# Three unread products beside each score transpose, in the stretch before the experts

## The reference, cut to what matters

```
x = layernorm(x + attention(x))                       # 16 heads, causal, 8 x 112 rows of 512
x = layernorm(x + gated_linear_attention(x, ctx))     # 8 x 375 context rows
logits = x @ router_weight.T + router_bias            # 8 experts
top_vals, top_idx = top_k(logits, 2)
scores = zeros.at[row, top_idx].set(softmax(top_vals))
act = (clip(up, -7, 7) + 1) * gate * sigmoid(1.702 * gate)      # per expert, 512 -> 2 x 512
expert_out = act @ down_proj[e] + down_proj_bias[e]             # 512 -> 512
out = sum over e of scores[:, e] * expert_out[e]
x = layernorm(x + out)
```

## Time and profile before

| | us |
|---|---|
| median of 3 runs | 919.36 |
| lowest and highest | 916.23, 919.87 |
| the profiled execution, its own time | 918.16 |
| its span, first to last instruction | 916.4 |
| TensorE busy in the span | 850.3 (93%) |
| mean granted TensorE clock | 0.964 |

### The profile page before, as it was taken

How to read it: one execution, slowest core, us unless ns; L and a number is a source line. 1 busy time by engine, 2 the same in 40 slices (tenths; PEclk the granted TensorE clock), 3 DMA queues, 4 the chain that set the end, 5 groups by cost and what they waited for, 6 DMA issues and landing times.

```text
span 916.4 us, 12580 instructions
## 1 busy us (share of the span) xinstructions
PE 850.3 (93%) x4967; PEld 743.9 (81%) x4967; DVE 470.6 (51%) x853; ACT 307.6 (34%) x666; POOL 105.6 (12%) x95
## 2 busy tenths in 40 slices
PE   6999999999999999899999999989988899999980
PEld 6999998989898989878898777777737888888760
DVE  4435454453636352756732335444665576666524
ACT  4343323141423332512542212221233355554420
POOL 0000000000000000000000001000131144444333
PEclk9999999999999999999999999999958899999995
DMA  9940725431200103004100101100564366655326
GB/s 327 351 161 1 236 77 188 126 123 64 87 6 25 69 1 116 1 6 167 35 1 1 34 34 58 58 1 24 217 231 120 122 188 187 190 154 165 72 30 184
DMA packets 34461, 96.99 MB, mean 106 GB/s; under 512 B 5720, under 2 KB 7768, under 8 KB 31712
## 3 DMA queue, kind: packets, MB, share of 16 engines
q1 hardware_dynamic: 30592, 87.70, 27.8%
q0 software_dynamic: 3808, 8.46, 4.6%
HBM read 64.03 MB, written 32.12 MB: 105 GB/s over the span
## 4 chain that ended last, share of the span: by engine, by line
PE 73%; issue 8%; DVE 8%; ACT 6%; POOL 2%; DMA 1%; SPq 0%; POOLq 0%; DVEq 0%; ACTq 0%
PE bank L278 58%; PE bank L600 3%; ACT w_gu L951 3%; PE bank L632 3%; PE bank L547 2%; POOL y_acc L472 2%; DVE hh L1708 1%; PE bank L734 1%; PE bank L590 1%; PE bank L523 1%; DVE prob L1281 1%; ACT x_g L1158 1%; PE bank L670 1%; DVE gl L1695 1%; PE bank L704 1%
## 5 line engine op out<-in xcount | busy, mean ns | idle before, releaser
L278 PE MATMUL bank<-w_kv,cT 128*125 128x512 f32 x576 | 145.0, 402 | 0.9 <-DVE acc L1270 0.9
L278 PE MATMUL bank<-xT,w_qkv 128*128 128x448 f32 x672 | 137.7, 365 | 0.0
L278 PEld LDWEIGHTS bank<-xT,w_qkv 128*128 128x128 f32 x672 | 126.1, 188 | 10.6 <-ACT qT L972 0.4
L278 PEld LDWEIGHTS bank<-w_kv,cT 128*125 128x125 f32 x576 | 104.7, 187 | 24.8 <-issue 1.3
L278 PE MATMUL bank<-x_g,w_gu 128*128 128x288 f32 x768 | 112.0, 305 | 6.0 <-issue 4.0
L278 PEld LDWEIGHTS bank<-x_g,w_gu 128*128 128x128 f32 x768 | 107.1, 195 | 9.4 <-issue 5.0
L278 PE MATMUL bank<-w_qkv,xT 128*112 128x256 f32 x672 | 85.3, 283 | 0.0
L422 POOL TENSOR_TENSOR ln_rs<-ln_ve,half 128x1 f32<-128x1 f32 (+2 forms) x16 | 12.6, 790 | 599.1 <-DVE ln_ve L1363 599.1
L278 PE MATMUL bank<-w_o,zT 128*128 128x512 f32 x336 | 79.8, 395 | 0.5 <-DVE acc L1558 0.5
L278 PEld LDWEIGHTS bank<-w_qkv,xT 128*112 128x112 f32 x672 | 79.9, 175 | 0.0
L278 PE MATMUL bank<-w_dn,hT 128*128 128x512 f32 (+1 forms) x288 | 70.2, 402 | 4.3 <-issue 4.3
(11 more groups left out here) (144 smaller groups left out, 1170.0 us busy)
## 6 DMA issues: line engine op xcount, KB each, us to landing
x_rows<-blank SPq DMA_DIRECT2D x9, 2084.0 KB, 19.6
raw_gu<-in_w_gu_dram SPq DMA_DIRECT2D x8, 2048.0 KB, 8.0
raw_w<-in_w_qkv_dram SPq DMA_DIRECT2D x21, 512.0 KB, 6.9
raw_dn<-in_w_down_dram SPq DMA_DIRECT2D x8, 1024.0 KB, 5.2
raw_c<-in_ctx_t_dram SPq DMA_DIRECT2D x8, 750.0 KB, 4.3
raw_o<-in_w_o_dram SPq DMA_DIRECT2D x8, 512.0 KB, 3.6
xg<-x_rows SPq DMA_DIRECT2D x8, 512.0 KB, 5.7
raw_kv<-in_w_kv_dram SPq DMA_DIRECT2D x2, 1024.0 KB, 6.9
```

Source lines behind the costliest of these rows:

```text
L278: last = nc.tensor.matmul(mm_out, lhs(a, k), rhs(b, k), start=(k == 0 and i == 0), stop=(k == n - 1 and i == 2))
```

## The change

A function `stay_awake` issues three matmuls on TensorE. All three have the same operands, a 128 x 128 and a 128 x 512 piece of `xT`, and all write bank 0, which nobody reads before a later product overwrites it. It is called for tiles 2 to 6 between `turn_score(n)` and `down_bias(n)`. One wait ahead of the loop makes sure that bank 0's last reader is done.

```diff
@@ -536,6 +536,10 @@
+            def stay_awake():
+                for _ in range(3):
+                    nc.tensor.matmul(banks[0][:, :], xT[:, 0, 0, 0:P], xT[:, 0, 0, 0:4 * P], start=True, stop=True)
@@ -854,8 +858,10 @@
             down_bias(1)
+            pe.wait_ge(free[0], LAST[0])
             for n in range(2, NT):
                 turn_score(n)
+                stay_awake()
                 down_bias(n)
```

## The result

| | before | after |
|---|---|---|
| median of 5 runs, us | 919.36 (914.29 to 919.87) | 924.08 (923.19 to 925.17) |
| ratio, 95% interval | | 1.0068 [1.0039, 1.0098] |
| the profiled execution: time, span | 918.16, 916.4 | 924.08, 922.2 |

The change makes the kernel slower by 4.7 us in the medians. The forecast was 917.1, and 924.08 lies just outside its range, which ended at 924.0. The case that came true is the first rival: the clock stays at half.

What follows compares the result with a forecast made beforehand. It took the half-clock chain of bias products before the experts as the bound. A returning clock would outweigh the added products and end the chain 2.3 us earlier: from 919.36 to 917.1 us, range 914.6 to 924.0.

Steps and rivals of the forecast that it cites:

- the first rival: Chain of bias products: 8-row matmuls leave the clock at half, chain grows 3.75 us, 923.1 us in all; chance 0.39.
- I give the return the better half: Chain of bias products: with idle gaps filled, full clock returns by the middle of the chain; chance 0.49.
- The rule on the clock gate: TensorE in the chain: the gate follows how busy the engine has lately been; by that alone the clock returns.
- The price at half clock: Each turn (score transpose, three added products, bias product): 3.47 us instead of 2.72, 0.75 more; 3.75 for five.
- The chain on the path: Bias products before the experts: each us put into or taken out of their chain moves the experts' start.
- The loads thus have 4.2 us of slack: First expert's row loads land at 684.3, bias chain ends at 688.48; no gain up to 4.2 us is eaten.
- keeps its length of 5.2 us: Stretch from the last bias product to the first expert product (687.68 to 692.87): unchanged by the change.
- The ±1.4 us for half clock in the experts: Expert products' start: half clock lasts 3.0 or 5.9 us, so up to 1.4 us lost or won; counted zero.
- At full clock: Each turn (score transpose, three added products, bias product) if the clock returns: 0.11 + 0.73 + 1.05 = 1.89 us.

Runs made afterwards that it cites:

- m2_rows128_nostay: Kernel before, no unread products, bias product replaced by a product of 128-row pieces of the row tile (bias left out); 911.64 us, one run.
- v1_zero_rows: Kernel before, complete, both bias product operands widened from 8 to 128 rows by zeros, no unread products; 912.51 us, ratio 0.9942.
- m3_eight_row_stay: Changed kernel with its fifteen unread products cut to 8 rows of both operands; 924.3 us, one run.
- v3_ahead: Kernel before with each score transpose issued one place earlier, ahead of the previous tile's bias product, nothing unread; 916.56 us, ratio 0.9981.
- m1_rows128: Changed kernel with the bias product replaced by a product of 128-row pieces of the row tile (bias left out); 914.98 us, one run.
- m5_stay_zero_rows: Changed kernel, complete, unread products kept, both bias product operands widened from 8 to 128 rows by zeros; 914.06 us, ratio 0.9961.
- m4_one: Changed kernel with one unread product in each group in place of three; 917.54 us, ratio 0.9998.

## Why the prediction was wrong, by its own steps

- **"I give the return the better half"** is the step that failed. Its ground was that the bias matmuls "occupy the engine as long as full ones would do", and that the gap of 0.34 us with the transpose beside it was all that set today's chain apart from the dense stretches. Both halves were tested. With the gap left in and the rows full, the clock returned (m2_rows128_nostay, v1_zero_rows). With the gap closed and 8 rows, it did not in 20 us (the changed kernel, m3_eight_row_stay). There was a second difference in the row, `8*128 8x512` against `128*128 128x512`. The prediction names it ("no row shows what such matmuls do for the clock without gaps") and then gives it no weight, since it calls the gap "the only thing" that sets the chain apart.
- **The rule on the clock gate.** The Trainium skill, TensorE: Matmul & The Clock Gate, Part 1, ties the gate to how busy the engine has been. The trace of the changed kernel does not agree if busy is read as the profile's busy time: 19.99 of 19.99 us at 0.50. The closing table's statement that a matmul with few rows takes as long as a full one does agree (2.07 us with 8 rows, 2.05 to 2.08 with 128); time in the array and effect on the clock are two things. Part 4's remark, that transposes do not count as busy in the same way, pointed the right way as an analogy, and no run here tests it for transposes.
- **The price at half clock** was 0.75 us a turn and measured 0.87, 3.75 against 4.35 in all. The mis-sized term is the start of the bias product: 0.22 + 1.25 = 1.47 us after the transpose was the estimate, 1.59 is measured. The pace of a product was right (0.42 against 0.43).
- **The rival** "the clock stays at half" gave 923.1, from 921.7 to 924.5, and 924.08 was measured. With 0.87 a turn it would have been 923.7. That rival was given 0.39, and the range above it stopped at 924.0 where its own bound was 924.5.
- **The chain on the path** was right, in both directions: 0.87 us more a turn moved the experts by 4.35, and 0.4 us less a turn (v3_ahead) by 2.3.
- **"The loads thus have 4.2 us of slack"** was right for the kernel before and did not hold where the chain got shorter. In m1_rows128 the transposes of the gathered rows started right at the landing, 11.8 us after the first transpose (686.11 - 674.27), and in the kernel before the rows had landed after 10.2 (684.3). So "no gain up to that size is eaten by them" was too hopeful: about 1.5 us were eaten of a gain of 4.5.
- **The tail "keeps its length of 5.2 us"**: 5.15.
- **The ±1.4 us for half clock in the experts**: 1.37 in the profiled execution. It can't be put down to the change. Over the ten kernels here whose first 48 expert products run in part at half clock they take from 7.93 us (m1_rows128) to 9.39, without order by the products in the chain.
- **At full clock** a turn with the products was to take 1.89 us. With full rows it took 1.66 (m1_rows128), a little cheaper than estimated: the pair of bias matmuls took 0.86 (677.48 to 678.34) where the estimate had 1.05. With 8 rows no run reached full clock in the chain.

## What to carry to other kernels

Before products are added to keep TensorE's clock up, look at the rows that its matmuls use there. Here a bias product over 8 rows filled TensorE and left the clock at half, and zeros in the other 120 rows, which cost TensorE nothing, brought it back and made the kernel 0.6% faster. Unread products pay where the engine idles for other engines and dense work follows (14 in a wait of 4.0 us), not between two links of the chain that sets the end: there each one beyond the idle hole is paid in full, at the slow clock. Count the hole first; here it held exactly one.

## What the runs showed of the hardware that was not expected

- TensorE was busy without a gap for 20 us at 0.50 with a mix of 8-row matmuls and full ones. With the same instructions and 128 rows in the bias product, 120 of them zeros, the granted clock was back at 1.00 within the first turn (m5_stay_zero_rows), and without the full products in the second (v1_zero_rows).
- The spells of half clock are not at the same place in each execution: a spell at 660.80 to 663.90 is in the changed kernel's profiled execution and not in that of before, over the same instructions. The same twelve products take 4.61 us in m3_eight_row_stay and 3.06 in m4_one, whose instructions are also the same up to there.
